# Residual of the last group of tiles on GpSimd, at the end of both expert stages

## The chip, the cores and the metric

One Trainium2 chip, one of its cores. The metric is the device time of one execution in microseconds; the kernel is a single launch. The engines are TensorE (PE), VectorE (DVE), ScalarE (ACT), GpSimd (POOL) and SyncE (SP, which only issues DMA here). They run their own instruction streams and meet at semaphores.

## The reference

The input `x` is 8 x 512 tokens of 128 numbers, 4096 rows, all float32. Six steps are added to it one after the other. Each begins with a layer norm of `x`:

```python
x = x + 0.5 * _L0_ffn_ref(_layernorm(x, axis=-1), ...)   # stage 0, "f"
x = x + _L0_attn_ref(_layernorm(x, axis=-1), ...)        # stage 1, "s": a linear recurrence over the sequence
x = x + 0.5 * _L0_ffn_ref(_layernorm(x, axis=-1), ...)   # stage 2, "f"
x = x + 0.5 * _L1_ffn_ref(_layernorm(x, axis=-1), ...)   # stage 3, "m": soft slots, 16 experts
x = x + _L1_attn_ref(_layernorm(x, axis=-1), ...)        # stage 4, "a": attention, 16 heads
x = x + 0.5 * _L1_ffn_ref(_layernorm(x, axis=-1), ...)   # stage 5, "m"
```

The change concerns the end of `_L0_ffn_ref`, a mixture of 8 experts of which each token uses the one with the highest gate probability:

```python
gate_probs = jax.nn.softmax(x @ gate_w.T, axis=-1)
expert_idx = jnp.argmax(gate_probs, axis=-1)
expert_w = jnp.take_along_axis(gate_probs, expert_idx[:, None], axis=1)[:, 0]
for e in range(n_experts):
    ye = jax.nn.relu(x @ w1[e] + b1[e]) @ w2[e] + b2[e]
    out = out + jnp.where((expert_idx == e)[:, None], ye * expert_w[:, None], 0.0)
```

So each token's new value is `x + 0.5 * probability * (its expert's row)`.

## The kernel before

`x` stays in SBUF for the whole kernel as 32 tiles of 128 tokens, `x[:, t, :]`. Tiles are counted in batches of 4 (`TB`, one sequence of 512, eight of them) and in groups of 8 (`GT`, four of them, g = 0 to 3). The stages run in the order of the string "fsfmam", and `s`, `m`, `f` functions give each engine its part of a stage.

An expert stage (`ffn`) normalises the tiles, writes them to DRAM, sorts the tokens by expert, gathers them back by GpSimd's indirect DMAs (L857), runs 39 pieces of work on TensorE, VectorE and ScalarE (L818, L744, L831, L689), and scatters each finished tile of results to its tokens' rows in DRAM (L863, GpSimd). When the last of the 32 scatters has landed, SyncE fetches the rows back in token order in four transfers, one for each group (L593), into `yback`; each has a semaphore `back[g]` of its own.

VectorE then goes through the groups in order (L715 on). For each it waits for `back[g]`, makes the residual with one `scalar_tensor_tensor` per tile (L718: row times probability plus `x`, 128x128, eight of them; `prob` already holds the factor 0.5), adds one to `x_done[n + 1]` for each, and goes on to the next stage's layer norm, `stats_after` (L483 on):

- `stats_take(g)`: `bn_stats` of each of the eight tiles (L448), then seven short operations on 128x8 (L453 to L462), of which L453, L454, L455, L457 and L458 have two operands in SBUF. The last one frees ScalarE's square root (L470).
- `stats_finish(g - 1)`: reciprocal and shift (L479, L480) of the group before, which release `ready`: from here the other engines may normalise that group. For the last group `stats_finish(g)` follows too.
- after a finish the next stage may hang in some work of its own (`after_finish`). Before the scan (stage 1) that is part of the normalisation of groups 2 and 3 (L516). Before the mixing (stage 3) it is the centring of some tiles (L984), and after group 1 the shift of group 0 (L991).

Where the mixing follows, the last group doesn't go to `stats_after` but to `take_last`: scale of group 0 for the unit vectors (`unit_vector`, L997 to L999, which waits for ScalarE's root L1188 over the eight squares L1183), shift of group 1 (L991), and then the statistics of group 3.

GpSimd has nothing to do from its last scatter to the first tiles of the next stage. In the scan it adds the vector D to `x` by batches (L910, 128x512); in the mixing it multiplies by gamma (L1146, 128x512) and by the unit scale (L1154, 128x512, the scale broadcast along the row). In the attention it does part of the rotations (L1834 to L1847, 128x512, each waiting for its own engine's result before it). GpSimd's part of stage 2 begins with a wait for all 32 of `x_done[2]`.

Of the kernel before, what the change touches and what calls it, by code (L numbers as in the profile page):

```python
# [17 lines left out]
ALU = mybir.AluOpType  # L18
# [3 lines left out]
P = 128  # L22
B, S, D = 8, 512, 128
T = B * S // P
TB = S // P
# [88 lines left out]
def build(nc, a, consts, rotary, out, xhat_dram, yrow_dram, stages="fsf"):  # L114
    ctx = ExitStack()
    with ctx:
        def sb(name, shape, dt=F32):
            return ctx.enter_context(nc.sbuf_tensor(name, shape, dt))

        def sem(name):  # L120
            return ctx.enter_context(nc.semaphore(name))
# [6 lines left out]
        x = sb("x", [P, T, D])  # L128
# [17 lines left out]
        def carve(area, at, shape, dt=F32):  # L146

            n = int(np.prod(shape)) * (2 if dt == BF16 else 4) // 4
            v = area[:, at:at + n]
            if dt != F32:  # L150
                v = v.bitcast(dt)
            names = "abcde"[:len(shape)]
            return v.rearrange(f"p ({' '.join(names)}) -> p {' '.join(names)}", **dict(zip(names[1:], shape[1:]))) if len(shape) > 1 else v
# [19 lines left out]
        r_t = carve(arena4, 1536, (8, T))  # L173
# [18 lines left out]
        yback = arena[:, 0:T * D].rearrange("p (t d) -> p t d", t=T)  # L192
# [80 lines left out]
        x_done = [sem(f"x_done{i}") for i in range(len(stages) + 1)]  # L273
# [154 lines left out]
        GT = 8  # L428
        GROUPS = T // GT
# [54 lines left out]
        def stats_after(dve, n, g):  # L484

            stats_take(dve, n, g)
            if g:
                stats_finish(dve, n, g - 1)
            if g == GROUPS - 1:
                stats_finish(dve, n, g)  # L490
# [4 lines left out]
        BY_SCALAR, BY_VECTOR = T - TB * (GROUPS - SHARED), TB * (GROUPS - SHARED)  # L495
# [23 lines left out]
        def normalise_scalar(act, n, s, at, stored=None, stored_at=None):  # L519
# [17 lines left out]
            for g in range(1, GROUPS):  # L537
# [3 lines left out]

        FFN_COUNTS = dict(v=0, normed=BY_SCALAR, normed_v=BY_VECTOR, turned=T, xT_ready=B, gated=B, log_ready=1, exp_ready=1,
                          one_ready=1, ranked=1, hot_ready=T, tile_ready=1, inverted=1, row_hot=1, lanes_ready=1, gather_ready=1, items_ready=1, cleared=1, g_turned=T,
                          xgT=T, h_mm=ITEMS, w1_ready=ITEMS, hT_ready=ITEMS, hT_ready_a=ITEMS, y_mm=ITEMS, y_ready=ITEMS)
        RING_COUNTS = dict(stored=[16 * 4] * 2, gathered=[16 * len(range(i, T, AHEAD)) for i in range(AHEAD)],
                           scattered=[16 * T], back=[16] * 4)
        ffn_sems = {k: sem(f"f_{k}") for k in FFN_COUNTS}
        ffn_rings = {k: [sem(f"f_{k}{i}") for i in range(len(v))] for k, v in RING_COUNTS.items()}  # L550
        chains = {"f": 0, "m": 0}

        def ffn(n):

            s, at = ffn_sems, {k: v * stages[:n].count("f") for k, v in FFN_COUNTS.items()}
            stored, gathered, scattered, back = (ffn_rings[k] for k in RING_COUNTS)
# [39 lines left out]
            def vector(dve):  # L596
# [9 lines left out]
                top, esum, prob, first, dest, lane, row, at_token = (r_t[:, k, :] for k in range(8))  # L606
# [106 lines left out]
                    result(j)  # L713

                for g in range(GROUPS):  # L715
                    dve.wait_ge(back[g], at["back"][g] + 16)
                    for t in range(GT * g, GT * g + GT):
                        nc.vector.scalar_tensor_tensor(x[:, t, :], yback[:, t, :], prob[:, t:t + 1], x[:, t, :],  # L718
                                                       ALU.mult, ALU.add).then_inc(x_done[n + 1], 1)
                    if g == GROUPS - 1 and n + 1 in last_take:  # L720
                        last_take[n + 1](dve)
                    else:
                        stats_after(dve, n + 1, g)
# [121 lines left out]
            def gpsimd(pool):  # L845

                if n:
                    pool.wait_ge(x_done[n], T)
                pool.memset(y_sorted[:], 0.0).then_inc(s["cleared"], 1)
                pool.wait_ge(s["gather_ready"], at["gather_ready"] + 1)  # L850
                for h in range(2):
                    pool.wait_ge(stored[h], at["stored"][h] + 16 * 4)

                def gather(t):
                    if t >= AHEAD:
                        pool.wait_ge(s["g_turned"], at["g_turned"] + t - AHEAD + 1)
                    pool.indirect_dma_start(xg[:, t % AHEAD, :], None, xhat_dram,  # L857
                                            bass.IndirectOffsetOnAxis(token_of[:, t:t + 1], 0)).then_inc(gathered[t % AHEAD], 16)

                def scatter(t):  # L860

                    pool.wait_ge(s["y_ready"], at["y_ready"] + t + E)
                    pool.indirect_dma_start(yrow_dram, bass.IndirectOffsetOnAxis(token_of[:, t:t + 1], 0),  # L863
                                            y_sorted[:, t * D:t * D + D], None).then_inc(scattered[0], 16)

                LATER = 10
                for t in range(AHEAD):
                    gather(t)
                for j in range(T + LATER):
                    if j + AHEAD < T:  # L870
                        gather(j + AHEAD)
                    if j >= LATER:
                        scatter(j - LATER)

            return dict(sync=sync, vector=vector, scalar=scalar, tensor=tensor, gpsimd=gpsimd)


        def scan(n):
# [40 lines left out]
            def tensor(pe):  # L919
# [29 lines left out]
                for b in range(B):  # L949
# [4 lines left out]
                    if b >= 4:  # L954
# [9 lines left out]
                          xT_ready=B, logit_c=2 * B, logit_d=2 * B, max_c=2 * B, max_d=2 * B, exp_c=T, exp_d=2 * B,  # L964
# [929 lines left out]


        kinds = {"f": ffn, "s": scan, "m": mix, "a": attention}
        parts = [kinds[k](n) for n, k in enumerate(stages)]
        block = ctx.enter_context(nc.Block())
# [56 lines left out]
```

## Time and profile before

| | |
|---|---|
| runs, median (lowest to highest) | 971.78 us (969.85 to 972.43), 3 runs |
| profiled execution, its own time | 971.89 us |
| its span on the core | 970.1 us |
| mean granted TensorE clock | 0.871 of full speed |
| end of stage 0: first landing of returned rows to scale of the last group | 154.3 to 177.3 us |
| end of stage 2: first landing of returned rows to TensorE's first work of stage 3 | 349.6 to 374.1 us |

A row of the page or of the timeline gives the start (us from the start of the span), the duration, the engine, the line of the kernel, the operation, what it writes and reads, and the count; rows with a count over one are merged, and the duration is then from the first start to the last end. In brackets stands how long the engine was idle before, and who released it. Where operations of one engine overlap a little in the pipeline, the start-to-start distance is shorter than the duration of one.

### The profile page before, as it was taken

How to read it: one execution, taken by the hardware profiler on the slowest of the kernel's cores; microseconds unless marked ns; L12 is line 12 of the kernel's file. 1: busy time of each engine (PE TensorE's matmuls, PEld its weight loads, DVE VectorE, ACT ScalarE, POOL GpSimd, SP SyncE). 2: the span in 40 equal slices, each digit the busy share in tenths (PEclk: the TensorE clock that was granted, in tenths of full speed). 3: DMA queues.
4: the chain of work that ended last, by engine and by line, in shares of the span. 5: the costliest groups of instructions: out<-in, count | busy, mean ns of one | idle time of the engine just before them, and what ended most of it. 6: DMA issues, size and time to landing. Idle time of an engine off the chain costs nothing.

```text
span 970.1 us, 18021 instructions
## 1 busy us (share of the span) xinstructions
PE 769.0 (79%) x5550; PEld 510.0 (53%) x5550; DVE 638.0 (66%) x2321; ACT 512.8 (53%) x1401; POOL 417.4 (43%) x537
## 2 busy tenths in 40 slices
PE   3779992987699914897929888889988999768977
PEld 3669991647499903675803233333333433346757
DVE  4555546685845468753797677777877886587534
ACT  4435542425255415865211576876767777558650
POOL 2046751301467524120376657668576633341200
PEclk9989995995599956999965698998989999969999
DMA  6741113002111130000043224122142200000002
GB/s 159 217 112 48 52 41 95 1 22 66 28 48 53 42 95 1 1 1 1 8 59 57 44 36 64 27 47 46 27 64 30 41 3 4 1 1 1 1 1 87
DMA packets 52525, 41.99 MB, mean 43 GB/s; under 512 B 9224, under 2 KB 48080, under 8 KB 52432
## 3 DMA queue, kind: packets, MB, share of 16 engines
q1 hardware_dynamic: 46784, 31.74, 16.3%
q0 software_dynamic: 4096, 8.40, 2.9%
q8 instruction: 47, 0.77, 0.3%
q10 hardware_dynamic: 1552, 0.70, 0.3%
q14 instruction: 46, 0.38, 0.2%
HBM read 17.35 MB, written 10.49 MB: 29 GB/s over the span
## 4 chain that ended last, share of the span: by engine, by line
PE 51%; DVE 17%; issue 10%; POOL 8%; ACT 7%; DMA 4%; SPq 2%; ACTq 1%; DVEq 0%; POOLq 0%
PE psum L818 8%; PE psum L831 7%; PE psum L1547 5%; PE psum L772 3%; PE psum L1532 3%; DVE cst L1614 2%; DVE half_stats L448 2%; DVE x L718 2%; PE psum L1318 2%; PE psum L1381 2%; PE psum L1281 2%; PE psum L1290 2%; PE psum L768 2%; PE psum L1487 2%; DVE arena L984 2%
## 5 line engine op out<-in xcount | busy, mean ns | idle before, releaser
L1614 DVE CUSTOM_DVE_ANT_0 cst<-psum,rot 128x512 bf16<-128x512 f32 (+3 forms) x512 | 219.1, 487 | 67.1 <-PE psum L1519 57.9
L1680 ACT ACTIVATE arena<-psum 128x512 f32<-128x512 f32 (+1 forms) x384 | 178.3, 529 | 52.1 <-PE psum L1532 46.6
L1519 PE MATMUL psum<-arena 48*128 48x512 bf16 (+3 forms) x512 | 121.5, 330 | 17.9 <-DVE row_max L1614 9.9
L1532 PE MATMUL psum<-arena 51*128 51x512 bf16 (+3 forms) x512 | 114.6, 315 | 10.9 <-ACT arena L1680 7.5
L744 ACT ACTIVATE arena<-psum,gate_b1T 128x128 f32<-128x128 f32 x234 | 69.0, 366 | 74.3 <-PE psum L818 74.3
L857 POOL DMA_INDIRECT arena<-xhat_rows,token_of x64 | 61.9, 967 | 104.9 <-DVE token_of L659 80.9
L1775 POOL TENSOR_SCALAR_AFFINE_SELECT arena<-arena 128x384 f32<-128x384 f32 x128 | 63.8, 523 | 96.5 <-ACT arena L1680 96.5
L1547 PE MATMUL psum<-arena 128*32 128x512 f32 (+3 forms) x1024 | 98.4, 482 | 7.6 <-POOL arena L1778 7.6
L818 PE MATMUL psum<-arena 128*128 x624 | 88.1, 286 | 4.5 <-issue 2.7
L831 PE MATMUL psum<-arena 128*128 x624 | 87.0, 283 | 0.5 <-ACT arena L744 0.5
L818 PEld LDWEIGHTS psum<-arena 128*128 128x128 f32 x624 | 79.1, 199 | 9.2 <-issue 8.9
L1532 PEld LDWEIGHTS psum<-arena 51*128 51x128 bf16 x512 | 38.6, 96 | 77.2 <-ACT arena L1680 45.9
L863 POOL DMA_INDIRECT result_rows<-arena,token_of x64 | 63.6, 994 | 32.5 <-DVE arena L689 22.2
L831 PEld LDWEIGHTS psum<-arena 128*128 128x128 f32 x624 | 76.3, 193 | 1.9 <-issue 0.9
L1519 PEld LDWEIGHTS psum<-arena 48*128 48x128 bf16 x512 | 38.9, 98 | 63.3 <-DVE row_max L1614 49.9
L689 DVE SCALAR_TENSOR_TENSOR arena<-psum,item_mask,arena 128x128 f32 x78 | 27.4, 351 | 53.3 <-PE psum L831 53.3
L470 ACT ACTIVATE st<-st 128x8 f32<-128x8 f32 x24 | 4.9, 208 | 106.8 <-DVE st L462 106.6
L1146 POOL TENSOR_TENSOR arena<-arena,gamma 128x512 f32<-128x512 f32 x16 | 22.4, 1402 | 55.9 <-DVE arena L984 35.6
L679 DVE TENSOR_SCALAR arena<-psum,gate_b1T 128x128 f32<-128x128 f32 x78 | 27.3, 350 | 27.9 <-PE psum L818 25.4
L1198 ACT ACTIVATE arena<-psum,neg_c 128x256 f32<-128x256 f32 x64 | 29.5, 473 | 27.4 <-DVE neg_c L1032 27.4
L448 DVE BATCH_NORM_STATS2 half_stats<-x 128x6 f32<-128x128 f32 x192 | 39.4, 278 | 6.7 <-DMA x<-in_L_attn_x 6.1
L1614 DVE DVE_READ_ACCUMULATOR2_ANT row_max<- 128x1 f32 x512 | 42.6, 83 | 0.0
(250 smaller groups left out, 1613.8 us busy)
## 6 DMA issues: line engine op xcount, KB each, us to landing
arena<-cut SPq DMA_DIRECT2D x192, 64.0 KB
xhat_rows<-xh SPq DMA_DIRECT2D x16, 256.0 KB, 2.3
arena<-result_rows SPq DMA_DIRECT2D x8, 512.0 KB, 6.1
x<-in_L_attn_x SPq DMA_DIRECT2D x4, 512.0 KB, 7.5
arena<-in_L_ffn_w SPq DMA_DIRECT2D x1, 2048.0 KB, 10.0
out<-x SPq DMA_DIRECT2D x4, 512.0 KB, 3.2
arena<-xhat_rows,token_of POOLq DMA_INDIRECT x64, 2.5
result_rows<-arena,token_of POOLq DMA_INDIRECT x64
```

What stands on the lines that cost most here:

```text
L448: nc.vector.bn_stats(half_stats[:, t, :], x[:, t, :]).then_inc(stat_sem, 1)
L744: last = nc.scalar.activation(hidT[:, j % 2, c, :], bank[4 + j % 2][:, c * P:c * P + P], ACT.Relu, bias=b1T[:, bass.ds(picked[j] * FC + c, ...
L818: last = pe.matmul(bank[(2 if c < BY_DVE else 4) + j % 2][:, c * P:c * P + P], w1_tile[:, j % 2, c * P:c * P + P], tokens, start=True, sto ...
L831: last = pe.matmul(bank[6 + j % 2][:, 0:D], hidT[:, j % 2, c, :], w2[:, bass.ds(e, 1), c, :], start=False, stop=(c == FC - 1))
L857: pool.indirect_dma_start(xg[:, t % AHEAD, :], None, xhat_dram, bass.IndirectOffsetOnAxis(token_of[:, t:t + 1], 0)).then_inc(gathered[t % ...
L863: pool.indirect_dma_start(yrow_dram, bass.IndirectOffsetOnAxis(token_of[:, t:t + 1], 0), y_sorted[:, t * D:t * D + D], None).then_inc(scat ...
L1519: mm = pe.matmul(to[:, col:col + (k + 1) * P], q_stack[b % STACKS][rows, h, k * P:k * P + P], k_stack[b % STACKS][rows, h, 0:(k + 1) * P], ...
L1532: mm = pe.matmul(bank[MAX_BANKS + number % EXP_BANKS][:, col:col + S - k * P], k_stack[b % STACKS][rows, h, k * P:k * P + P], q_stack[b % ...
L1547: last = pe.matmul(bank[6][32 * j:32 * j + 32, k * P:], v_aug[b % 2][:, k, HALF * a + h, :], prob_e[g % 2][:, j, E_AT[k]:E_AT[k] + S - k * ...
L1614: last = nc.vector.tensor_tensor_reduce(masked_scores[:, number % 2, col:col + n_keys], frm[:, col:col + n_keys], mask[:, S - n_keys:], 1. ...
L1680: nc.scalar.activation(prob_e[g % 2][:, j, first:last], bank[MAX_BANKS + number % EXP_BANKS][:, 0:last - first], ACT.Exp, scale=DH ** -0.5 ...
L1775: pool.affine_select(blocks, blocks, pattern=[[0, 3], [1, P]], compare_op=ALU.is_ge, fill=0.0, base=0, channel_multiplier=-1)
```

## The change

The loop over the groups on VectorE no longer makes the residual of the last group (g = 3, batches 6 and 7). In its place VectorE waits until `rows_added` has gone up by two, and then raises `x_done[n + 1]` by eight at once. GpSimd, after its last scatter, waits for `back[3]` and does for each of the two batches a multiply of the returned rows by the probabilities (in place, 128x512, the probability broadcast along the row), a wait for its own result, and an add to `x`. Two semaphores are added, with their counts. The groups 0 to 2 are treated as before. It applies to stages 0 and 2.

```diff
-        FFN_COUNTS = dict(v=0, normed=BY_SCALAR, ...
+        FFN_COUNTS = dict(v=0, rows_scaled=2, rows_added=2, normed=BY_SCALAR, ...
...
                 for g in range(GROUPS):
-                    dve.wait_ge(back[g], at["back"][g] + 16)
-                    for t in range(GT * g, GT * g + GT):
-                        nc.vector.scalar_tensor_tensor(x[:, t, :], yback[:, t, :], prob[:, t:t + 1], x[:, t, :],
-                                                       ALU.mult, ALU.add).then_inc(x_done[n + 1], 1)
+                    if g == GROUPS - 1:
+                        dve.wait_ge(s["rows_added"], at["rows_added"] + 2)
+                        dve.sem_inc(x_done[n + 1], GT)
+                    else:
+                        dve.wait_ge(back[g], at["back"][g] + 16)
+                        for t in range(GT * g, GT * g + GT):
+                            nc.vector.scalar_tensor_tensor(x[:, t, :], yback[:, t, :], prob[:, t:t + 1], x[:, t, :],
+                                                           ALU.mult, ALU.add).then_inc(x_done[n + 1], 1)
                     if g == GROUPS - 1 and n + 1 in last_take:
                         last_take[n + 1](dve)
                     else:
...
                     if j >= LATER:
                         scatter(j - LATER)
+
+                pool.wait_ge(back[GROUPS - 1], at["back"][GROUPS - 1] + 16)
+                for k, b in enumerate((B - 2, B - 1)):
+                    rows, tiles = yback[:, TB * b:TB * b + TB, :], x[:, TB * b:TB * b + TB, :]
+                    prob = r_t[:, 2, TB * b:TB * b + TB].unsqueeze(2).to_broadcast([P, TB, D])
+                    pool.tensor_tensor(rows, rows, prob, ALU.mult).then_inc(s["rows_scaled"], 1)
+                    pool.wait_ge(s["rows_scaled"], at["rows_scaled"] + k + 1)
+                    pool.tensor_tensor(tiles, tiles, rows, ALU.add).then_inc(s["rows_added"], 1)
```

## Rows read from the trace of the kernel before

**Rows 1.** The page, section 1: busy time, share of the span, instructions.

```profile
PE 769.0 (79%) x5550; PEld 510.0 (53%) x5550; DVE 638.0 (66%) x2321; ACT 512.8 (53%) x1401; POOL 417.4 (43%) x537
```

**Rows 2.** The chain that ended last, 140 to 200 us: start, us, what.

```profile
154.30 2.20 DVE x L718 x8
...
170.09 2.11 DVE x L718 x8
```

**Rows 3.** The same view, 342 to 400 us.

```profile
349.60 2.20 DVE x L718 x8
...
367.75 4.12 DVE x L718 x8
```

**Rows 4.** Timeline, end of stage 0, VectorE, group 1: start, us, engine, line, operation.

```profile
159.13 2.18 DVE L718 SCALAR_TENSOR_TENSOR x<-arena,x 128x128 f32<-128x128 f32 x8
...
161.34 1.64 DVE L448 BATCH_NORM_STATS2 half_stats<-x 128x6 f32<-128x128 f32 x8
163.02 0.17 DVE L453 TENSOR_TENSOR st<-half_stats 128x8 f32<-128x8 f32 x1
...
163.47 0.16 DVE L457 SCALAR_TENSOR_TENSOR st<-st 128x8 f32<-128x8 f32 x1
...
164.18 0.17 DVE L480 SCALAR_TENSOR_TENSOR st<-st 128x8 f32<-128x8 f32 x1
```

**Rows 5.** Transfers of the returned rows, end of stage 2: first and last start; issue to landing.

```profile
L593 SPq DMA_DIRECT2D arena<-result_rows x4: 360/680/1952, 345.4 to 347.3; - x4
...
DMA to landing us min/median/max: 4.2/6.1/7.6
```

**Rows 6.** GpSimd's groups: duration min/median/max in ns; busy, mean ns, idle before.

```profile
L1154 POOL TENSOR_TENSOR xh<-arena,st x2: 1040/1041/1042, 377.8 to 383.3; 128x512 f32<-128x512 f32 x2
...
L1841 POOL TENSOR_TENSOR raw<-raw,arena 128x512 f32<-128x512 f32 x15 | 19.6, 1305 | 0.7
```

**Rows 7.** Timeline, end of stage 2, from 360 us: VectorE, then GpSimd.

```profile
360.19 2.19 DVE L718 SCALAR_TENSOR_TENSOR x<-arena,x 128x128 f32<-128x128 f32 x8
...
361.48 2.02 POOL L1146 TENSOR_TENSOR arena<-arena,gamma 128x512 f32<-128x512 f32 x1 [17.37 <-ACT arena L1173]
```

**Rows 8.** Timeline, end of stage 2, from 367.6 us: VectorE and GpSimd.

```profile
367.66 4.20 DVE L718 SCALAR_TENSOR_TENSOR x<-arena,x 128x128 f32<-128x128 f32 x8
...
367.67 1.46 POOL L1146 TENSOR_TENSOR arena<-arena,gamma 128x512 f32<-128x512 f32 x1 [2.94 <-ACT arena L1173]
...
369.10 1.31 POOL L1146 TENSOR_TENSOR arena<-arena,gamma 128x512 f32<-128x512 f32 x1
...
369.20 1.35 DVE L718 SCALAR_TENSOR_TENSOR x<-arena,x 128x128 f32<-128x128 f32 x1
```

**Rows 9.** Timeline: VectorE beside GpSimd, in stage 1 and in stage 3.

```profile
166.18 2.73 POOL L910 TENSOR_TENSOR x<-x,arena 128x512 f32<-128x512 f32 x2 [17.31 <-ACT xh L530]
...
166.48 1.65 DVE L448 BATCH_NORM_STATS2 half_stats<-x 128x6 f32<-128x128 f32 x8
...
168.16 0.78 DVE L453 TENSOR_TENSOR st<-half_stats 128x8 f32<-128x8 f32 x1
...
377.81 1.00 DVE L480 SCALAR_TENSOR_TENSOR st<-st 128x8 f32<-128x8 f32 x1
```

**Rows 10.** Timeline, end of stage 0, around the scales of groups 1 and 2.

```profile
169.92 0.17 DVE L480 SCALAR_TENSOR_TENSOR st<-st 128x8 f32<-128x8 f32 x1
...
171.85 2.81 POOL L910 TENSOR_TENSOR x<-x,arena 128x512 f32<-128x512 f32 x2 [2.94 <-ACT xh L530]
...
173.22 1.10 ACT L534 COPY xT<-psum 128x512 f32<-128x512 f32 x2
...
175.87 1.65 ACT L530 ACTIVATE xh<-x,st 128x128 f32<-128x128 f32 x4
```

**Rows 11.** Timeline, end of stage 2, the root of group 0 and its taker.

```profile
370.83 0.21 ACT L1188 ACTIVATE st<-st 128x8 f32<-128x8 f32 x1
...
371.79 0.16 DVE L997 TENSOR_SCALAR st<-st 128x8 f32<-128x8 f32 x1
```

More of the change, by code:

```diff
@@ L540, in normalise_scalar @@
             tiles(GROUPS - 1)
-        FFN_COUNTS = dict(v=0, normed=BY_SCALAR, normed_v=BY_VECTOR, turned=T, xT_ready=B, gated=B, log_ready=1, exp_ready=1,
+        FFN_COUNTS = dict(v=0, rows_scaled=2, rows_added=2, normed=BY_SCALAR, normed_v=BY_VECTOR, turned=T, xT_ready=B, gated=B, log_ready=1, exp_ready=1,
                           one_ready=1, ranked=1, hot_ready=T, tile_ready=1, inverted=1, row_hot=1, lanes_ready=1, gather_ready=1, items_ready=1, cleared=1, g_turned=T,
```

## The prediction

> **What bounds the kernel now.** I read four views in this order. First the busy times of the page: no engine is full (TensorE 79%, VectorE 66%, GpSimd 43%), so the work moved here is worth only what the chain of waits says [rows 1]. Then the chain in order of time, at the two places where the changed loop runs, the ends of stages 0 and 2 (I call them site 1 and site 2). At both, VectorE is the chain from the landing of the first quarter of the returned rows: residual, statistics, residual, statistics, and the residual of the last group of tiles is on it: 2.11 us at 170.09, and 4.12 us at 367.75 [rows 2, 3]. GpSimd is idle there until the next stage's first tiles are normalised (17.3 us at either site; the timeline gives it in brackets behind its next instruction) [rows 7, 9]. So at first sight 2.1 + 4.1 = 6.2 us leave the chain. The rest of the reading says what of this is left, and what GpSimd's new work does to VectorE's.
>
> **Part 1, when GpSimd's four operations run.** The last quarter is issued at 347.3 and lands 7.6 us later, at 354.9; at site 1 the same view gives 152.4 and 7.2, 159.6 [rows 5]. Both instants lie 0.4 to 0.5 us inside VectorE's eight residual operations of group 1 (159.13 to 161.31) [rows 4]. GpSimd then does multiply, add, multiply, add on 128x512. The multiply by a broadcast column is the operation of L1154, 1.04 us; the add of two full tensors is priced by L1841 of the attention, 1.305 us in the mean of 15, which also waits for its own engine's result before it, 0.7 us idle for the 15, 0.05 each [rows 6]. The four take 2 x 1.04 + 2 x 1.305 + 3 x 0.05 = 4.8 us: over at 164.5 undisturbed, or at about 166 after waiting for VectorE's stream to end. VectorE asks for the result at 170 (site 1) and 367.7 (site 2), so the new wait on `rows_added` costs nothing: its cover is 4 to 6 us. Nothing but the `sem_inc` and the statistics stands behind that wait. GpSimd's own next instruction, L910 at 166.18, is freed by group 0's normalised tiles; it moves with VectorE, not with the four operations.
>
> **Part 2, what the four operations cost VectorE.** VectorE's statistics of the tiles don't feel GpSimd: 1.65 us for eight beside a running L910, 1.64 without [rows 4, 9]. Its operations with two operands in SBUF do. L453, 0.17 us, takes 0.78 and ends with L910; L480, 0.17 us, takes 1.00 beside an L1154 [rows 4, 9]. The residual itself has two: at 367.66 its eight take 4.20 us beside two L1146, 2.02 more than 2.18, so 1.01 for each GpSimd operation [rows 8]. So one met operation costs 0.83 us (multiply) or 1.01 us (add), and how many are met depends on who gives way. The rows show both. At 361.48 GpSimd's L1146 came into a running stream of residuals and took 2.02 instead of 1.3: it ended 1.12 us after the stream's end (362.38), so it had waited it out, and the stream was at its full speed, 2.19 [rows 7]. At 367.67 it broke in after one [rows 8].
> *GpSimd waits the stream out.* Operation 1 lies under the statistics from 161.3; operation 2 ends at 163.6, so that L453, due at 163.02, ends at 163.6 instead of 163.19 (0.41); operation 3 ends at 164.70 and holds L457, then due at 163.88, to 164.72 instead of 164.04 (0.68); operation 4 ends at 166.06 and holds L480, then due at 165.27 (0.65) [rows 4]. Sum 1.75 us.
> *GpSimd breaks in, and two residuals pass between its operations.* The stream's last five or six meet three operations, the fourth falls under the statistics: 0.83 + 1.01 + 0.83 = 2.7 us.
> *It breaks in and one passes between:* all four are met, 3.7 us.
> I take 2.2 us for a site, the middle of the first two (one site each way gives the same): GpSimd's waits on its own results leave VectorE time for a second residual (its starts are 0.26 us apart), where the two back-to-back L1146 left time for one. Bounds: 0 (nothing met) and 3.7. All of it is in front of group 0's or group 1's scale, for which ScalarE, GpSimd and TensorE wait idle, so it is paid in full: +4.4 us for both.
> The Trainium skill ("SBUF — State Buffer", "Who interferes with whom") speaks against this change: VectorE operations with two SBUF inputs and GpSimd operations that read SBUF exclude each other, and the one issued first holds the port for its whole instruction. By that rule GpSimd would break in behind the running residual, the second or third case, and a site would cost 2.7 to 3.7. The 2.02 us of 361.48 disagree, the 4.20 us of 367.66 agree.
>
> **Part 3, what leaving out the last residual gives back.** Site 1: let R be the scale of group 1 (L480 ends at 170.09). Today group 2's is at R + 5.75 (175.84). ScalarE, which takes it up at 175.87, is busy from R with group 1's eight tiles and two copies until 174.32, R + 4.2, so no more than 1.5 us can be gained [rows 10]. Without the residual the statistics run from R - 0.1 to R + 1.6; but the L910 pair, which R's normalised tiles release at R + 1.76 and which now falls under statistics, then falls on the short operations: L457 is held to R + 3.1 by the first, L480 to R + 4.45 by the second. Gain 5.75 - 4.45 = 1.3 us (bounds 1.0 and 1.5). So the chain's 2.11 us is not had.
> Site 2: behind the residual is L997, which needs ScalarE's root of group 0; L1188 gives that at 371.04. VectorE arrives at 371.79 today and would arrive at 367.75 [rows 11]. The root's own chain (centring, eight squares) hangs on group 1's scale, which isn't sooner. Gain 0.7 us; the other 3.4 of the 4.12 turn into a wait for L1188. Bounds 0.6 and 0.75.
> Together 2.0 us. Since it cannot be above 2.25, even a change without any cost stays below what a measurement of this kernel tells from no change (0.3%, 2.9 us).
>
> **Sum.** 2 x 2.2 - 2.0 = +2.4 us on the profiled execution's 971.89: 974.3. The median of the runs is 971.78, 0.11 lower: 974.2. Both later chains (the scan; the slot mixing) start from the delayed scales with idle engines, so I expect nothing to absorb it.
>
> **Rivals.**
> A, slower: GpSimd breaks into the residuals of group 1 at both sites and lets one pass at a time. For it: 367.66. Against it: 361.48, and the waits between its operations. 2 x 3.7 - 2.0 = +5.4, 977.2; at one site alone, +3.9, 975.7. Where it decides: from about 2.5 us per site on, the result is slower by more than 0.3%.
> B, nearly free: the four operations fall under the statistics, or the blocked operations aren't those on the chain. For it: statistics make up 1.64 of each 4.8 us round. Against it: the operations take 4.8 us, three times that stretch. -2.0 us, 969.8.
> C, even: only one or two are met, about 1 us a site, as much as is gained: 971.8. For it: L910 and L1146, two at a time, cost VectorE only some 0.6 us where the first lies under the statistics, as L453's 0.78 for 0.17 [rows 9].
> D, slower: GpSimd breaks in at both sites, two residuals pass each time: 2 x 2.7 - 2.0 = +3.4, 975.2. For it: 367.66 [rows 8] and the waits between its operations; against it: 361.48 [rows 7]. It is what the skill's rule of the exclusive port gives.
> That the change doesn't do what it says (VectorE still waiting at `rows_added`) has 5 us of cover against it and almost no chance.
>
> **How the numbers follow.** Forecast, with the stream waited out at one site at least, 0.43, its own range 2 x 1.75 - 2.0 to 1.75 + 3.7 - 2.0, that is 973.3 to 975.2. D 0.14; A 0.20; B 0.11; C 0.12. Slower by over 0.3% (above 974.7): A and D whole, and 0.05 of the forecast, 0.39. Faster by over 0.3% (below 968.9): only if something unseen adds to B, 0.05. Within: 0.56. The range from 970.0 to 977.6 takes in the forecast, C, D, most of A and the edge of B.
>
> **What would show each step.** GpSimd's new operations start at 159.6 and 354.9, of 1.04 and about 1.3 us. Right: at both sites two or three operations of VectorE (residuals of group 1, L453, L457, L480) of about 1 us, and group 0's scale later by 1.8 to 2.7 us; behind R two blocked short operations; at site 2 VectorE idle for some 3 us in front of L997. Wrong: residuals of group 1 with four of 1.0 to 1.4 us (A); no long ones (B); an add far above 1.3 us, or GpSimd still at it when VectorE comes to the wait, which would need it to end 4 us late.

## The result, and the profile after

The changed kernel takes 977.92 us (median of 5 runs, 976.68 to 978.99) against 971.78 us of the kernel before: ratio 1.0062, 95% interval 1.0049 to 1.0076. That is 6.1 us slower, where 2.4 us were forecast and 970.0 to 977.6 given as the range. The profiled execution of the changed kernel took 976.68 us, with a span of 974.9 us. One execution of the last run below, 1125.12 us at a granted clock of 0.639, is in none of the figures of that run.

The page, section 1, of the changed kernel: GpSimd is busy 9.1 us more, VectorE 2.4 us more although sixteen of its operations are gone [rows 1].

```profile
span 974.9 us, 18015 instructions
...
PE 767.3 (79%) x5550; PEld 508.3 (52%) x5550; DVE 640.4 (66%) x2305; ACT 512.5 (53%) x1401; POOL 426.5 (44%) x545
```

The chain that ended last, 350 to 380 us, is the quickest way to the cause. The eight residuals of group 1 (L722 now) stand in it with 5.83 us. The last group's, 4.12 us before [rows 3], are gone, and in their place the chain runs over ScalarE: centring (L1185), root (L470), squares (L1195), root (L1200).

```profile
352.28 2.20 DVE x L722 x8
...
357.19 5.83 DVE x L722 x8
...
366.67 2.11 DVE x L722 x8
...
372.32 2.42 ACT arena L1185 x6
374.74 0.10 ACT st L470
374.84 2.35 ACT arena L1195 x16
377.21 0.22 ACT st L1200
377.45 0.18 DVE st L1009
```

The timeline of the changed kernel at site 1 answers to [rows 4]: first VectorE, then GpSimd. The eight residuals of group 1 take 5.97 us (2.18 before). GpSimd's four operations, L883 the multiply and L885 the add, lie side by side with them.

```profile
158.99 5.97 DVE L722 SCALAR_TENSOR_TENSOR x<-arena,x 128x128 f32<-128x128 f32 x8
164.99 1.65 DVE L448 BATCH_NORM_STATS2 half_stats<-x 128x6 f32<-128x128 f32 x8
...
159.53 1.03 POOL L883 TENSOR_TENSOR arena<-arena 128x512 f32<-128x512 f32 x1 [10.70 <-DMA arena<-result_rows]
160.64 1.26 POOL L885 TENSOR_TENSOR x<-x,arena 128x512 f32<-128x512 f32 x1
161.86 1.09 POOL L883 TENSOR_TENSOR arena<-arena 128x512 f32<-128x512 f32 x1
163.03 1.26 POOL L885 TENSOR_TENSOR x<-x,arena 128x512 f32<-128x512 f32 x1
```

Narrow windows of the same timeline show which residuals are held; each line is two neighbours, from the start of the first to the end of the second. Those that start at 159.52, 160.63, 161.97 and 163.02 take 1.19, 1.42, 1.12 and 1.41 us in place of 0.34, and each ends about 0.15 us behind one of GpSimd's operations.

```profile
159.25 1.46 DVE L722 SCALAR_TENSOR_TENSOR x<-arena,x 128x128 f32<-128x128 f32 x2
159.52 2.54 DVE L722 SCALAR_TENSOR_TENSOR x<-arena,x 128x128 f32<-128x128 f32 x2
160.63 2.46 DVE L722 SCALAR_TENSOR_TENSOR x<-arena,x 128x128 f32<-128x128 f32 x2
161.97 2.46 DVE L722 SCALAR_TENSOR_TENSOR x<-arena,x 128x128 f32<-128x128 f32 x2
```

At site 2 it is the same picture, four of GpSimd's operations in eight residuals:

```profile
357.10 5.90 DVE L722 SCALAR_TENSOR_TENSOR x<-arena,x 128x128 f32<-128x128 f32 x8
...
357.89 1.24 POOL L883 TENSOR_TENSOR arena<-arena 128x512 f32<-128x512 f32 x1 [11.02 <-DMA arena<-result_rows]
```

Group L722 of the changed kernel, durations min/median/max in ns. The median is the undisturbed 343; the longest took 1419 (344 and 1355 for the same group of the kernel before, the 1355 being the 1.35 us of [rows 8]).

```profile
L722 DVE SCALAR_TENSOR_TENSOR x<-arena,x x48: 338/343/1419, 154.2 to 368.4; 128x128 f32<-128x128 f32 x48
```

What comes back behind group 1's scale (L480 at 173.57, ended 173.74) at site 1: the statistics follow at once, but the pair of L922 (L910 before) now meets L455 and L458, and holds each to its own end. In the kernel before it met L453 alone, which took 0.79 us.

```profile
173.57 0.17 DVE L480 SCALAR_TENSOR_TENSOR st<-st 128x8 f32<-128x8 f32 x1
173.69 1.65 DVE L448 BATCH_NORM_STATS2 half_stats<-x 128x6 f32<-128x128 f32 x8
...
175.55 1.25 DVE L455 TENSOR_TENSOR st<-half_stats 128x8 f32<-128x8 f32 x1
...
177.11 1.22 DVE L458 TENSOR_TENSOR st<-st 128x8 f32<-128x8 f32 x1
...
178.67 0.17 DVE L480 SCALAR_TENSOR_TENSOR st<-st 128x8 f32<-128x8 f32 x1
...
175.50 1.27 POOL L922 TENSOR_TENSOR x<-x,arena 128x512 f32<-128x512 f32 x1 [2.94 <-ACT xh L530]
177.04 1.27 POOL L922 TENSOR_TENSOR x<-x,arena 128x512 f32<-128x512 f32 x1 [0.27 <-ACT xh L530]
```

And at site 2 VectorE now waits 3.3 us for the root before L1009 (L997 before; compare [rows 11]):

```profile
377.45 0.17 DVE L1009 TENSOR_SCALAR st<-st 128x8 f32<-128x8 f32 x1 [3.32 <-ACT st L1200]
```

Each site can be balanced on its own clock, from the first residual on. From the first residual to the scan's first VectorE operation (L887 of the kernel before) it was 30.39 us and is 33.52: +3.13. To TensorE's first work of stage 3 it was 24.49 and is 27.48: +2.99. Together 6.1 us, and the medians differ by 6.1. The spans of the two profiled executions differ by only 4.8 us: outside the two sites that of the changed kernel is 1.3 us shorter. From TensorE's first work of stage 3 to the end, the fourteen traces of this case take 594.8 to 598.1 us, so a single span doesn't tell such a difference; the local figures do.

### The profile page after: what moved, and what is told of

It reads as the page before. It is cut to its first block, busy times and chain, and to the rows that moved or that the text cites. A ratio compares the mean times of both kernels' runs of the same rounds, so it can differ in the third digit from the quotient of the medians.

```text
span 974.9 us, 18015 instructions
## 1 busy us (share of the span) xinstructions
PE 767.3 (79%) x5550; PEld 508.3 (52%) x5550; DVE 640.4 (66%) x2305; ACT 512.5 (53%) x1401; POOL 426.5 (44%) x545
## 4 chain that ended last, share of the span: by engine, by line
PE 50%; DVE 19%; issue 10%; ACT 8%; POOL 8%; DMA 2%; ACTq 1%; DVEq 0%; SPq 0%; POOLq 0%
PE psum L822 8%; PE psum L835 7%; PE psum L1559 5%; PE psum L776 3%; DVE half_stats L448 3%; DVE cst L1626 3%; PE psum L1544 2%; DVE x L722 2%; PE psum L1499 2%; PE psum L1330 2%; PE psum L1393 2%; PE psum L1293 2%; PE psum L1302 2%; DVE arena L996 2%; PE psum L1531 2%
## 5 line engine op out<-in xcount | busy, mean ns | idle before, releaser
L470 ACT ACTIVATE st<-st 128x8 f32<-128x8 f32 x24 | 4.9, 208 | 113.5 <-DVE st L462 113.3
L1286 PE MATMUL psum<-cst,xh 128*128 128x128 f32 x64 | 10.7, 293 | 40.9 <-POOL xh L1166 40.9
```

## The experiments

Local figures below are differences to the kernel before, taken in the same way: at site 1 from the first residual to L887, at site 2 from the first residual to TensorE's first work in stage 3. They are worked out from starts in the traces, one profiled execution each. The medians of the kernel before, measured beside them, were 971.0 to 971.7 us.

| run | ratio to before (95%) | median us | site 1, local | site 2, local |
|---|---|---|---|---|
| changed kernel | 1.0062 (1.0049 to 1.0076) | 977.92 | +3.13 | +2.99 |
| last residual left out | 0.9989 (0.9980 to 0.9999) | 970.73 | -0.63 | -0.72 |
| GpSimd's load only | 1.0075 (1.0059 to 1.0092) | 978.49 | +3.81 | +3.84 |
| memsets instead | 0.9996 (0.9982 to 1.0009) | 970.94 | -0.62 | -0.51 |
| behind group 1's residuals | 1.0047 (1.0030 to 1.0064) | 975.66 | +1.95 | +1.87 |
| site 1 only | 1.0037 (1.0020 to 1.0054) | 974.26 | +3.07 | 0.00 |
| site 2 only | 1.0028 (1.0012 to 1.0044) | 974.12 | 0.00 | +2.99 |
| 0.2 us later | 1.0068 (1.0049 to 1.0088) | 977.35 | +3.07 | +3.01 |
| GpSimd only adds | 1.0011 (0.9998 to 1.0023) | 972.36 | -0.14 | -0.22 |
| ScalarE scales groups 1, 2 | 0.9983 (0.9969 to 0.9997) | 969.40 | -1.24 | -1.66 |
| the same, and group 3 at site 2 | 0.9970 (0.9957 to 0.9983) | 967.77 | -1.28 | -2.29 |
| adds of D late | 0.9990 (0.9977 to 1.0003) | 970.21 | -1.23 | -0.01 |
| both of the last | 0.9964 (0.9952 to 0.9977) | 967.49 | -3.02 | -2.28 |

**The last residual left out.** What can the change give at best?

```diff
-                        dve.wait_ge(s["rows_added"], at["rows_added"] + 2)
+                        dve.wait_ge(back[g], at["back"][g] + 16)
                         dve.sem_inc(x_done[n + 1], GT)
...
-                pool.wait_ge(back[GROUPS - 1], at["back"][GROUPS - 1] + 16)
-                for k, b in enumerate((B - 2, B - 1)):
-                    ...
```

> The residual of the last group is left out at both sites: VectorE waits for the last quarter of the rows and raises x_done, GpSimd has no new work (the output lacks the expert rows of tiles 24 to 31). Theory 1 (the port is the cost, and the residual on VectorE was worth little): what the change can gain at best, 0.65 to 1.3 us at site 1 and 0.7 us at site 2, so 971.8 - 1.4 to - 2.0 = 969.8 to 970.4 us. Theory 2 (the chain of waits read literally): 2.1 + 4.1 = 6.2 us less, 965.6.

970.73 us, by the ratio 1.1 us less, locally 0.63 and 0.72. The chain read literally, 6.2 us, is refuted. All of its group's residuals are as fast as they can be:

```profile
L722 DVE SCALAR_TENSOR_TENSOR x<-arena,x x48: 342/344/352, 154.1 to 361.0; 128x128 f32<-128x128 f32 x48
```

With nothing new on GpSimd, the scale of group 2 comes 5.10 us behind that of group 1 here too (169.88 and 174.98, ends of L480; 5.75 before): it is the pair L910, not the four operations, that takes half of the 1.3 us that I had counted.

**GpSimd's load only.** VectorE's program is that of the kernel before; the four operations run on the free gather buffer.

```diff
+                pool.wait_ge(back[GROUPS - 1], at["back"][GROUPS - 1] + 16)
+                for k in range(2):
+                    low, high = xg[:, 0:TB, :], xg[:, TB:2 * TB, :]
+                    prob = r_t[:, 2, 0:TB].unsqueeze(2).to_broadcast([P, TB, D])
+                    pool.tensor_tensor(low, low, prob, ALU.mult).then_inc(s["rows_scaled"], 1)
+                    pool.wait_ge(s["rows_scaled"], at["rows_scaled"] + k + 1)
+                    pool.tensor_tensor(high, high, low, ALU.add).then_inc(s["rows_added"], 1)
+                    pool.wait_ge(s["rows_added"], at["rows_added"] + k + 1)
```

> The kernel before, VectorE's work unchanged, plus the four GpSimd operations of the same shape on scratch rows at the same time, for which nobody waits. Theory 1: the eight residuals of group 1 take about 5.9 us instead of 2.2 at both sites, 2 x 3.75 = 7.5 us more, 979.3 us. Theory 2 (the loss came from the new wait and the later x_done, not from the port): no change, 971.8 us.

978.49 us, +7.2 by the medians, locally +7.65. The cost is there in full without the new wait, without the late `x_done` and on other addresses. The longest residual is the 1419 ns of the changed kernel:

```profile
L718 DVE SCALAR_TENSOR_TENSOR x<-arena,x x64: 337/345/1419, 154.1 to 378.9; 128x128 f32<-128x128 f32 x64
```

**Memsets instead.** The same places, operations that only write; as in the first run, the residual of the last group is left out.

```diff
-                    pool.tensor_tensor(rows, rows, prob, ALU.mult).then_inc(s["rows_scaled"], 1)
...
+                    rows = yback[:, T - GT:T, :]
+                    pool.memset(rows, 0.0).then_inc(s["rows_scaled"], 1)
```

(and likewise for the add, with a wait for its own result behind it)

> GpSimd's four operations are replaced by four memsets of 128x1024 that only write (about 0.9 us each by the memset of 128x4096, 3.5 us); the residual of the last group is left out. Theory 1a (only reads collide, as the Trainium skill has it, SBUF - State Buffer, Who interferes with whom): the residuals of group 1 stay at 2.2 us, and the time is that of the kernel with the residual left out, about 970 us. Theory 1b (any GpSimd operation in SBUF keeps VectorE off): four blocks of 0.7 to 0.9 us at a site, 2 x 3.2 - 1.4 = +5, 977 us.

970.94 us, as with the residual left out. At site 1 two of the four memsets, 0.95 us each, lie over the residuals of group 1, and these take 2.18 us; the other two lie over the statistics and the short operations:

```profile
159.09 2.18 DVE L722 SCALAR_TENSOR_TENSOR x<-arena,x 128x128 f32<-128x128 f32 x8
...
159.60 0.95 POOL L882 MEMSET arena<- 128x1024 f32 x1 [10.69 <-DMA arena<-result_rows]
160.60 0.95 POOL L884 MEMSET arena<- 128x1024 f32 x1
```

So GpSimd's writing doesn't keep a two-operand VectorE operation off, and what is left of the operations is their reading; theory 1a holds. (A GpSimd operation that reads one operand alone was not run.) By the Trainium skill ("SBUF — State Buffer", "Who interferes with whom") a VectorE instruction with two SBUF inputs collides with a GpSimd instruction that reads SBUF, not with one that only writes: this run agrees. One short operation did feel the memsets, the `tensor_scalar` L456: 0.44 us at site 2 and 0.25 at site 1 in place of 0.17. The same section counts `tensor_scalar` among the operations that can take both ports.

**Behind group 1's residuals.** The number and kind of GpSimd's operations stay, only their time changes.

```diff
                 pool.wait_ge(back[GROUPS - 1], at["back"][GROUPS - 1] + 16)
+                pool.wait_ge(x_done[n + 1], 2 * GT)
```

> The changed kernel, but GpSimd also waits until VectorE has done the residuals of group 1 (x_done at 16) before its four operations. Theory 1: the first operation and most of the second fall under the statistics; L453, L457, L480 are held, 1.75 us a site in place of 3.75; 971.8 + 3.5 - 1.4 = 973.9 us, 4 us under the changed kernel. Theory 3 (the cost hangs on how many operations run, not on when): unchanged, 977.9 us.

975.66 us, 2.3 us under the changed kernel where 4 were expected. The intervals of the two ratios overlap; the local figures say the same 2.3. The cost of a site falls from 3.8 to 2.6 us (group 0's scale, L480, ends 12.6 us behind the first residual; 10.05 before, 13.8 in the changed kernel), so timing matters (theory 3 falls), but by less than worked out. Three short operations are held, as expected, but L453, L455 and L457, and for 0.67, 0.84 and 1.07 us, 2.6 in place of 1.75. The statistics beside the first two of GpSimd's operations take 1.64 us, as without them.

```profile
163.21 0.84 DVE L453 TENSOR_TENSOR st<-half_stats 128x8 f32<-128x8 f32 x1
163.98 0.16 DVE L454 TENSOR_TENSOR st<-half_stats 128x8 f32<-128x8 f32 x1
164.06 1.01 DVE L455 TENSOR_TENSOR st<-half_stats 128x8 f32<-128x8 f32 x1
165.11 0.17 DVE L456 TENSOR_SCALAR st<-st 128x8 f32<-128x8 f32 x1
165.19 1.23 DVE L457 SCALAR_TENSOR_TENSOR st<-st 128x8 f32<-128x8 f32 x1
```

**One site at a time.** Site 1 only (n == 0, shown), then site 2 only (n == 2); the other as before.

```diff
-                    if g == GROUPS - 1:
+                    if g == GROUPS - 1 and n == 0:
...
+                if n == 0:
                     pool.wait_ge(back[GROUPS - 1], at["back"][GROUPS - 1] + 16)
```

> The change at site 1 alone (stage 0); stage 2 as before. Theory 1 with the traces of before and after: the residuals of group 1 cost 3.8 more, 0.65 us comes back behind group 1's scale: +3.1, 974.5 us. Rival (the two sites share one cost, such as code that is loaded once): nearly all of the 6 us here, 977.5, or none.

> The change at site 2 alone (stage 2); stage 0 as before. Theory 1: 3.7 more in the residuals of group 1, 0.7 back in front of L997: +3.0, 974.4 us. Rival as for site 1 alone.

974.26 and 974.12 us, +3.07 and +2.99 locally, nothing at the other site. The two add up.

**0.2 us later.** Does it depend on the instant within VectorE's step whether GpSimd breaks in?

```diff
                 pool.wait_ge(back[GROUPS - 1], at["back"][GROUPS - 1] + 16)
+                pool.memset(xg[:, 0, 0:48], 0.0)
```

> The changed kernel with a memset of 128x48 on GpSimd between the wait for the last quarter and the first operation: the first operation comes some 0.2 us later within the 0.26 us step of VectorE's residuals. In the row of 361.48 GpSimd came 0.23 us behind a start and 0.03 us before the next one, and gave way to the whole stream; in the new rows it came 0 to 0.02 us behind a start and broke in. Theory P (the phase decides): with about 0.23 us GpSimd gives way at one site or both, which then cost 2.8 us as in the gated run, not 3.75: 975.7 to 977 us. Theory O (the operation or its place decides): no difference, 977.9 us or 0.2 less.

977.35 us. The first reading operation now comes 0.19 and 0.11 us behind the start of a residual, against 0.01 and 0.00, and breaks in all the same; the groups take 5.90 us at both sites. The phase I aimed at, 0.23, was missed, so theory P isn't excluded for it, but it is no lever. Why L1146 at 361.48 waited the stream out stays open. In all ten other traces that keep the residuals of group 2 as they were it does so again, at the same place in the stream, with 2.00 to 2.04 us. In the three where group 2's residual is two adds, it comes as they end and takes 1.26 us.

**GpSimd only adds.** ScalarE multiplies the last group's rows, GpSimd is left with two operations of the four.

```diff
+                act.wait_ge(back[GROUPS - 1], at["back"][GROUPS - 1] + 16)
+                for t in range(T - GT, T):
+                    nc.scalar.activation(yback[:, t, :], yback[:, t, :], ACT.Copy, scale=r_t[:, 2, t:t + 1]).then_inc(s["rows_scaled"], 1)
...
-                    pool.tensor_tensor(rows, rows, prob, ALU.mult).then_inc(s["rows_scaled"], 1)
-                    pool.wait_ge(s["rows_scaled"], at["rows_scaled"] + k + 1)
+                    pool.wait_ge(s["rows_scaled"], at["rows_scaled"] + TB * (k + 1))
                     pool.tensor_tensor(tiles, tiles, rows, ALU.add).then_inc(s["rows_added"], 1)
```

> Half the dose: ScalarE multiplies the last group's rows by the probabilities (eight activations, 0.29 us apart as the last run showed), GpSimd makes only the two adds, VectorE nothing, at both sites. Theory 1 (each GpSimd operation that meets a two-operand one of VectorE costs its own time): two operations in place of four, the first beside the end of the residuals of group 1 (1.0 us or 0), the second mostly under the statistics (0.3 to 0.6 us); 0.3 to 1.6 us a site, less 1.4 us that leaving out the residual gives back: 971.0 - 0.8 to + 1.8 = 970.2 to 972.8 us. Rival (the cost is one of GpSimd being awake at all): as the changed kernel, 977.

972.36 us, no measurable difference to the kernel before (its interval reaches from -0.2 to +2.2 us; locally -0.4). The first add comes at the last residual (160.94), takes 1.49 us in place of 1.26, so it seems to wait for it, and then lies under the statistics, as does nearly half of the second. Of VectorE's operations only L453 is held, 0.66 us. So what the four operations cost hangs on what they meet, and two that meet next to nothing cost next to nothing; the run is no measure of half the meetings.

```profile
163.01 0.66 DVE L453 TENSOR_TENSOR st<-half_stats 128x8 f32<-128x8 f32 x1
...
160.94 2.71 POOL L886 TENSOR_TENSOR x<-x,arena 128x512 f32<-128x512 f32 x2 [12.15 <-ACT arena L767]
```

**ScalarE scales groups 1 and 2.** An engine beside which VectorE's operations keep their length in this trace (statistics of 1.64 us under ScalarE's sixteen activations, 156.28 to 161.06), and groups whose residual is on the chain in full.

```diff
+                for g in (1, 2):
+                    act.wait_ge(back[g], at["back"][g] + 16)
+                    for t in range(GT * g, GT * g + GT):
+                        nc.scalar.activation(yback[:, t, :], yback[:, t, :], ACT.Copy, scale=r_t[:, 2, t:t + 1]).then_inc(s["rows_scaled"], 1)
...
+                    if g in (1, 2):
+                        for b in (2 * g, 2 * g + 1):
+                            dve.wait_ge(s["rows_scaled"], at["rows_scaled"] + TB * (b - 1))
+                            tiles = x[:, TB * b:TB * b + TB, :]
+                            nc.vector.tensor_tensor(tiles, tiles, yback[:, TB * b:TB * b + TB, :], ALU.add).then_inc(x_done[n + 1], TB)
```

> Another engine in GpSimd's place, and other groups: ScalarE, which is idle there and shares no port with VectorE in these traces, multiplies the rows of groups 1 and 2 by the probabilities in place (eight activations of 128x128, 0.385 us apart, 3.1 us a group), and VectorE adds them with two adds of 128x512 (0.60 us apart by L991) in place of eight residuals (2.18 us). Groups 0 and 3 as before, GpSimd has no new work. Theory 1: 0.98 us a group leaves the chain, in front of scales for which the others wait, at both sites: 4 x 0.98 = 3.9 us less, 967.9 us. Rival (the square root of group 0 now stands behind ScalarE's sixteen activations, until 162.4 at site 1, and holds the scale of group 0): half of it, 969.8 us, or nothing.

969.40 us, ratio 0.9983 (0.9969 to 0.9997): faster, by less than the 3.9 us worked out. A group's residual falls from 2.18 to 1.29 us, 1.78 for the two groups of a site. At site 2 0.13 of it is lost, because L453 is held a little longer (0.79 for 0.66). At site 1 the adds of D fall elsewhere: one has L456 take 1.28 us in place of 0.17, and L453 is nearly free of them (0.21 in place of 0.78), which leaves 1.24. ScalarE's table load, 1.28 us, which the kernel before has in idle time (145.73), now stands behind the activations and in front of the square root of group 0. It costs nothing here: the root ends at 162.59, and VectorE takes it up at 163.25, straight behind its own L462.

**Group 3 too, at site 2.**

```diff
+            on_act = (1, 2, 3) if stages[n + 1] == "m" else (1, 2)
...
+                    if g == GROUPS - 1:
+                        stats_root(act, n + 1, 0)
```

> As the run with ScalarE scaling groups 1 and 2, and at site 2 group 3 too, behind the square root of group 0, VectorE adding it with two adds of 128x512. Theory 1: the residual of group 3 at site 2 is worth 0.7 us at most, since L997 then waits for the root of the squares (368.70 in that run, against 369.46 of VectorE): 968.7 us. Rival (the 4.2 us residual is on the chain as drawn): 3 us less, 966.5.

967.77 us, ratio 0.9970 (0.9957 to 0.9983). L997's counterpart comes 19.81 us behind the first residual, 20.53 in the run before it: 0.72 us for a residual that had stood in the chain with 4.1 (0.63 up to TensorE's first work). Again VectorE only waits longer for the root:

```profile
364.74 1.28 DVE L722 TENSOR_TENSOR x<-x,arena 128x512 f32<-128x512 f32 x2
368.14 0.25 DVE L1012 TENSOR_SCALAR st<-st 128x8 f32<-128x8 f32 x1 [2.12 <-ACT st L1203]
```

**The adds of D late.** The kernel before, its own collision taken away.

```diff
-                    wait_normed(pool, s, at, TB * b + TB - 1)
+                    if b == 0:
+                        pool.wait_ge(s["normed"], BY_SCALAR)
+                        pool.wait_ge(s["normed_v"], BY_VECTOR)
```

> The kernel before with GpSimd's eight adds of D in the scan (L910) behind the last normalised tile instead of beside VectorE's statistics; they are needed only from about 200 us. Theory 1: L453 is held 0.6 us in each of two groups, and the normalisation L516 about 1 us by the same adds; 1.2 to 2.2 us less, 969.2 us. Rival (the adds then end too late or collide with the scan on VectorE, which reads PSUM): no change or slower.

970.21 us, ratio 0.9990, within the measurement; locally 1.23 us less, twice the 0.6 us of L453, which is back at 0.17 us. The 1 us at L516 isn't to be had: it is 1.11 in place of 2.24 us long, and the scan starts no sooner for it (6.24 us behind L516's start in both).

```profile
168.09 0.17 DVE L453 TENSOR_TENSOR st<-half_stats 128x8 f32<-128x8 f32 x1
...
177.15 1.11 DVE L516 TENSOR_SCALAR xh<-x,st 128x128 f32<-128x128 f32 x4 [1.16 <-PE psum L927]
```

**Both together.** ScalarE's scaling with group 3 at site 2, and the adds of D late.

> ScalarE scaling (groups 1 and 2, at site 2 also 3) and the adds of D late, together. Theory 1: the two add up and more, since in the ScalarE run one add of D held L456 for 1.28 us: 971.0 - 2.4 - 1.5 to 2.5 = 966.5 us. Rival (both take the same idle time, ScalarE is the bound at site 1): 968.5.

967.49 us, ratio 0.9964 (0.9952 to 0.9977): faster than both kernels, by 0.4% than the one before and by 1% than the changed one, and not to be told from the run without the late adds. At site 1 the two help each other (3.02 us, against 1.28 and 1.23): no short operation is held any more, so the two adds give their whole 1.78 us and L453 1.23. Locally it is 5.3 us, in the medians 4.2 and in the ratio 3.5: part of it isn't seen at the end. In its profiled execution TensorE's first work of stage 3 to the end took 598.1 us against 596.0 before, the longest of the fourteen traces (594.8 to 598.1); whether that is more than their scatter is open.

## Why the prediction was wrong, point by point

**What was right.** That 6.2 us of the chain are not to be had, and why: in front of L997 the root takes over at site 2 (0.7 us worked out, 0.72 measured with the residual left out), and no version of the change can gain 2.25 us. The run with the residual left out settles it. Right too: when the four operations start (5.4 and 5.6 us behind the first residual, where 5.3 was forecast), how long they are, that nobody waits at `rows_added`, that the statistics don't feel them (1.64 us in the gated run), and nearly the price of one meeting: 0.78 to 0.85 us for a multiply and 1.08 for an add, read from the residuals of 1.12 and 1.19 us and of 1.41 and 1.42 against 0.34 (0.83 and 1.01 were taken).

**The step that failed** is the count of meetings, the 2.2 us for a site in part 2. I had three cases from two rows that disagreed, and took the middle of the two cheaper ones. It was the third: GpSimd broke in at both sites and one residual passed between its operations, so all four were met, 3.79 and 3.72 us. The reason I gave for two passing residuals, that GpSimd's waits on its own results leave VectorE time, was a guess, and it failed: there are two such waits, not the three of part 1, only 0.07 to 0.09 us long each, and the residual held by the last operation is still running when the next one starts (at 160.64 that of 159.52 runs until 160.71). The load-only run shows the same 3.8 us with nothing else changed. The first case was also priced too low: in the gated run, where GpSimd comes behind the residuals, a site costs 2.6 us and not 1.75, so even a forecast built on that case alone, with the measured gains, would have been some 975.6 us (971.8 + 2 x 2.6 - 1.35).

**The second error** is smaller: the gain at site 1 was given as 1.3 us with a lower bound of 1.0, and is 0.65. I had the pair of D adds hold L457 and L480. It comes 0.05 us before L455 (175.50 and 175.55), so L455 and L458 are held, each for a whole operation: R + 5.10 in place of R + 4.45. The bound was too narrow, because I bounded by ScalarE and not by the case in which both adds are met in full. The rows of the pair in front of me had L453 held for 0.79 us only because it met the rest of one.

**The sum with the measured terms** is 3.79 + 3.72 - 0.65 - 0.72 = 6.1 us, and the medians differ by 6.1. Rival A, worked out at 977.2 us and given 0.20, is what happened (977.9); it lacks 0.65 us at site 1 and 0.1 in the two counts. The upper end of the range lay only 0.4 us above A's own number, though A too had an uncertain gain to subtract; that left the measured time 0.3 us outside. That the result is slower at all was no luck: the meetings forecast as its cause are its cause, but there were more of them.

**The rule of the Trainium skill** ("SBUF — State Buffer", "Who interferes with whom"; D, and with one residual passing A) pointed the right way: one of the two engines blocks the other for a whole instruction, and each meeting here cost nearly a whole one. It says nothing on how many residuals pass, so it doesn't choose between D and A. On its issue order this trace doesn't decide: the residual of 159.52 was held by an operation of GpSimd that starts at 159.53. I weighed one row against it, 361.48, as if it were half of the evidence. That row is real and comes back in the other traces. It is the same pair of operations as 367.66 (L1146 beside L718), and the only one of the two in which GpSimd came into a running stream, so leaving it out would not have been sound either: what decides whether GpSimd waits the stream out or breaks in is open, and the new operations broke in in all eight groups that they met.

## What to carry to other kernels

An operation moved from VectorE to GpSimd is not hidden by being early: as long as it reads SBUF beside two-operand VectorE operations, each GpSimd operation adds nearly its whole length to VectorE. Count meetings, not engine idle time, and before moving anything look for what is late next behind the operation: leaving it out altogether showed 0.63 and 0.72 us where the chain drew 2.1 and 4.1. Work split off to ScalarE had no such price, only that it moved the adds of D onto L456 at site 1, and gained most on the groups whose residual is in front of every wait.

## What the runs showed of the hardware that I had not expected

- With both engines asking, they alternated one for one, even where GpSimd's next operation waited for its own result: the eight residuals took 5.90 to 6.03 us with four GpSimd operations in all eight groups that met all four (the changed kernel, the load-only run, the one-site runs and the shifted one), whether the first came 0.00 or 0.19 us behind a start.
- A VectorE operation held in this way shows as busy, not as idle: VectorE's busy time rose by 2.4 us while it had sixteen operations fewer.
- ScalarE's activations of 128x128 without a bias follow each other by 0.29 us (L774, sixteen in 4.78 us, in the run with group 3 too), those with bias and scale (L530) by 0.385.

```profile
350.14 4.78 ACT L774 ACTIVATE arena<-arena 128x128 f32<-128x128 f32 x16 [10.29 <-DMA arena<-result_rows]
```
